# A wait on GpSimd for VectorE's attention shift, in a fused decoder layer on one core

## The reference

```python
# 1: linear attention, 32 heads of 8
qkv = relu(x @ W_qkv.T); q, k, v = split(qkv)
vk = [v | 1]^T k ;  z = vk q ;  y = (z[:8] / (z[8] + 1e-15)) @ W_p.T + b_p
x = layernorm(x + y)
# 2: cross attention to a context (16, 256, 256), 16 heads of 16, 2D rotary positions
q = rope(x @ Wq.T); k = rope(c @ Wk.T); v = c @ Wv.T
x = layernorm(x + softmax(q k^T / 4) v @ Wo.T + b_o)
# 3: low-rank feed-forward, 256 -> 64 -> 1024 -> 64 -> 256
x = layernorm(x + gelu(x @ U1 @ V1 + b1) @ U2 @ V2 + b2)
```

## Time and profile before

| | |
|---|---|
| median of three executions | 564.23 us |
| the profiled execution | 563.59 us |
| its span | 561.7 us |
| TensorE busy (matmuls) | 501.4 us, 89% of the span |
| VectorE busy | 427.0 us, 76% |
| GpSimd busy | 343.9 us, 61% |
| ScalarE busy | 312.5 us, 56% |
| mean granted TensorE clock | 0.967 of full speed (2.4 GHz) |

### The profile page before, as it was taken

How to read it: one execution, slowest core, us unless ns; L and a number is a source line. 1 busy time by engine, 2 the same in 40 slices (tenths; PEclk the granted TensorE clock), 3 DMA queues, 4 the chain that set the end, 5 groups by cost and what they waited for, 6 DMA issues and landing times.

```text
span 561.7 us, 11399 instructions
## 1 busy us (share of the span) xinstructions
PE 501.4 (89%) x4044; PEld 338.6 (60%) x4044; DVE 427.0 (76%) x878; ACT 312.5 (56%) x457; POOL 343.9 (61%) x391
## 2 busy tenths in 40 slices
PE   6997899998989898989898989898969678999992
PEld 3885666666676666666666767575746234545451
DVE  6567778888888888888888888888887767254554
ACT  3552366574647474747373747465646457656560
POOL 6558064858585867676767677676667334433435
PEclk9999799999999999999999999999999689999997
DMA  8553103011311132021203120302000001133332
GB/s 274 142 99 103 43 12 81 16 57 34 75 51 43 39 72 82 11 54 58 84 8 55 58 81 11 90 22 61 11 25 11 25 20 57 39 112 113 114 113 112
DMA packets 29131, 36.01 MB, mean 64 GB/s; under 512 B 5720, under 2 KB 15320, under 8 KB 29080
## 3 DMA queue, kind: packets, MB, share of 16 engines
q1 hardware_dynamic: 28216, 34.37, 21.6%
q10 hardware_dynamic: 864, 0.95, 0.6%
HBM read 23.51 MB, written 8.65 MB: 57 GB/s over the span
## 4 chain that ended last, share of the span: by engine, by line
PE 64%; DVE 17%; issue 9%; POOL 4%; ACT 4%; DMA 1%; POOLq 1%; SPq 0%; ACTq 0%
PE FR L1222 18%; PE BK L1222 12%; PE BK L1400 8%; PE SC L1381 5%; PE SC L1349 5%; DVE nmax L1037 5%; PE FR L1309 4%; PE FR L1301 3%; DVE shift L1047 3%; DVE nmax_c L1043 3%; PE FR L1286 3%; PE FR L1426 2%; POOL rs L647 2%; POOL c_fm L652 2%; DVE lin_fm_l L996 2%
## 5 line engine op out<-in xcount | busy, mean ns | idle before, releaser
L1037 DVE TENSOR_REDUCE nmax<-SC 128x4 f32<-128x1024 f32 x128 | 155.6, 1216 | 25.8 <-PE SC L1349 24.6
L755 ACT ACTIVATE probs<-SC 128x1024 f32<-128x1024 f32 x128 | 130.9, 1026 | 68.6 <-PE SC L1381 68.4
L1400 PE MATMUL BK<-probs,v_aug 128*32 128x256 f32 x1024 | 70.2, 393 | 0.3 <-DVE y L1087 0.3
L1349 PE MATMUL SC<-k_blk,q_grp 48*128 48x512 f16 x256 | 51.4, 398 | 7.9 <-DVE nmax L1037 7.0
L1381 PE MATMUL SC<-q_grp,k_blk 64*128 64x256 f16 x512 | 50.9, 279 | 5.2 <-ACT probs L755 2.5
L851 ACT ACTIVATE probs<-SC,b_ff 128x512 f32<-128x512 f32 x64 | 38.9, 688 | 25.9 <-PE SC L1591 25.9
L536 POOL TENSOR_TENSOR rs<-ve,minus_half 128x2 f32<-128x2 f32 x16 | 11.3, 706 | 52.5 <-DVE nm L1019 52.5
L1400 PEld LDWEIGHTS BK<-probs,v_aug 128*32 128x32 f32 x1024 | 27.0, 110 | 27.1 <-issue 12.3
L1381 PEld LDWEIGHTS SC<-q_grp,k_blk 64*128 64x128 f16 x512 | 20.0, 96 | 32.6 <-issue 15.4
L717 ACT ACTIVATE lin_fm_h<-FR 128x512 fp32r<-128x512 f32 x15 | 9.0, 597 | 46.0 <-PE FR L1309 46.0
L529 POOL TENSOR_TENSOR att_fm_l<-att_raw,att_fm_h 128x512 fp32r<-128x512 f32 x16 | 20.6, 1288 | 20.7 <-ACT att_fm_h L730 20.7
(11 more groups left out here) (239 smaller groups left out, 1588.4 us busy)
## 6 DMA issues: line engine op xcount, KB each, us to landing
x_fm<-in_x_fm SPq DMA_DIRECT2D x16, 256.0 KB, 5.9
x_tm<-in_x_tm SPq DMA_DIRECT2D x16, 256.0 KB, 5.4
x_kept<-x2b SPq DMA_DIRECT2D x16, 256.0 KB, 2.1
x_tm<-x_kept SPq DMA_DIRECT2D x16, 256.0 KB, 2.7
out<-c_fm SPq DMA_DIRECT2D x16, 256.0 KB, 2.0
c_fm<-in_c_fm SPq DMA_DIRECT2D x15, 256.0 KB, 5.3
tables<-rope_tables SPq DMA_DIRECT2D x16, 128.0 KB
k_blk<-k_rope SPq DMA_DIRECT2D x128, 16.0 KB, 1.8
```

Source lines behind the costliest of these rows:

```text
L755: act.activation(probs[:, j % 4], (SC[j % 2] if b == LAST else SB)[:], ACT.Exp, scale=SCALE).then_inc(s_exp, 1)
L1037: dve.tensor_reduce(nmax[:, t, :, 2 * q:2 * q + 2], src[:].rearrange("p (s f) t -> p s f t", s=2), AX.X, ALU.max, negate=True).then_inc(s_ ...
L1349: mm = pe.matmul(out[:, 2 * s:2 * s + 2].rearrange("p h t -> p (h t)"), q_grp[n % NB][rows, q, t * P:(t + 1) * P], k_blk[n % NB][rows, q]. ...
L1400: mm = pe.matmul(BK[q // 2][HP * k:HP * (k + 1), (q % 2) * T:(q % 2 + 1) * T], v_aug[b % NB][:, t, HC * q + k], probs[:, j % 4, k], start= ...
```

## The change

One line is added to GpSimd's step. After the last instruction of `rope_q(n)`, GpSimd waits until s_shift has reached b + 2, that is, until VectorE has finished shift(b+1) at the end of its own step b. Only then does it go on with `residual2(n)`, `keep_x2(q)` and `split_c(m)`. In steps without a block n (b = 14) there is no wait.

```diff
@@ -587,6 +587,7 @@
                     split_x(m + 1)
                 if on(n):
                     rope_q(n)
+                    pool.wait_ge(s_shift, b + 2)
                     residual2(n)
                 if on(q):
                     keep_x2(q)
```

## The result

| | before | changed |
|---|---|---|
| median of the first comparison | 563.96 us (4 runs) | 535.75 us (4 runs) |
| the changed kernel again, on another chip | 564.66 us (11 runs) | 537.50 us (6 runs) |
| the profiled execution | 563.59 us | 537.56 us |
| its span | 561.7 us | 535.8 us |
| ratio | | 0.9506, 95% interval 0.9481 to 0.9532; again: 0.9507, 0.9472 to 0.9542 |

The change makes the kernel 4.9% faster. The profiled execution lost 26.03 us; the medians lost 28.2 and 27.2. The prediction had 537.5 us, 26.1 less than the profiled execution before.

A forecast was written before the change was run, and what follows sets the result against it. The loop was bound by TensorE's queue plus one wait for VectorE's shift, held by GpSimd. Idle 24.5 plus overlap 2.1 less 0.5 for ve made 26.1 us, off the profiled 563.59: 537.5 us, range 533.5 to 545.

The forecast's parts named there:

- The rival that the shift is slow for a reason of its own: VectorE's shift: GpSimd contention is not the cause, so no change, 563.6 us; chance 0.02.
- The sum: Whole run: 24.5 us of TensorE idle plus 2.1 of overlap less 0.5 gives 26.1 us won.
- 0.15: TensorE, each of 14 changed steps: us won beyond the idle, because queued matmuls overlap; 2.1 us in all.
- ve's 0.5: VectorE's L1018 (128x2), held by GpSimd's cs_fm_l: 0.4 to 0.5 us late, counted in full once, behind b = 12.
- the spacing of the two score groups: TensorE: last scores start 0.23 us after block n1's first; the transposes should follow equally, so a step gains 2.07.
- The nearest row: VectorE's L1092 at 475.32, beside GpSimd's lin_tm: 0.34 instead of 0.17 us, so L1018 should also wait for GpSimd's end.
- The tail: GpSimd's held-back x1b, x2b, cs_fm_h and cs_fm_l: 4.46 us, running 273.80 to 278.26 behind the shift.
- The covers: Slack behind held work: costs 0; rs's 2.71 us just used up, VectorE's PSUM copy not held, ScalarE's copy 0.4 early.
- the rival of half a us a step: A hold reaches TensorE every step through L1018 or ScalarE's normalization: gain 20, time 543.5 us; chance 0.13.
- the one that all of VectorE's work is held: GpSimd's tail holds all VectorE work behind the shift: 0.4 us a step left, 558 us; chance 0.05.
- The slower rival: Shift, GpSimd's tail, rs, normalization, transposes become the loop once the tail takes 6.9 us; at 7.5, 572 us; chance 0.03.
- The clock: TensorE's clock falls near the end: if gone, 1 to 4 us more, outside the sum; 531 to 535, chance 0.09.

The follow-up runs named there:

- e2: Against the kernel before: the new wait one instruction later, behind x1b (residual2), leaving one GpSimd instruction beside the shift; 545.5 us, ratio 0.9694.
- e4: Against the kernel before, no wait: x1b and x2b each written by two 128x256 instructions instead of one 128x512; 549.96 us, ratio 0.9769.
- e1: Against the kernel before: the new wait behind split_c, so all four GpSimd instructions still run beside the shift; 564.23 us, ratio 1.0017.
- e3: Against the kernel before: the new wait behind keep_x2, leaving two GpSimd instructions (x1b, x2b) beside the shift; 558.7 us, ratio 0.9922.
- e6: Changed kernel with three extra unread 128x512 GpSimd additions behind x2b in steps b = 2 to 12; 564.26 us, ratio 1.0 to the kernel before.
- e7: Changed kernel with 30 extra unread matmuls in TensorE's waits of the last three steps, first run; 535.62 us, ratio 0.95 to the kernel before.
- e8: Apparently (by the order of the text) the changed kernel unaltered, run again on another chip; 537.50 us, ratio 0.9507 to the kernel before.

## Why the prediction was right

**The cause.** The shift's three operations each wait for the end of GpSimd's instruction in hand: shown by e2 to e4, with one, two, and half instructions beside them. The rival that the shift is slow for a reason of its own fell with them. That the wait itself does something is ruled out by e1, and by e3, where it held GpSimd and won no more than the one free operation. Which resource VectorE and GpSimd contend for no run here shows.

**The sum, part by part.** Every stretch between two transposes can be held against the one before. TensorE's transposes before that stand in no group above, then those after:

```profile
61.81 0.39 PE L1365 MATMUL FR<-ident,shift 128*128 128x128 f16 x2
...
111.84 0.29 PE L1365 MATMUL FR<-ident,shift 128*128 128x128 f16 x2 [0.91 <-DVE shift L1049]
...
385.78 0.28 PE L1365 MATMUL FR<-ident,shift 128*128 128x128 f16 x2 [1.92 <-DVE shift L1049]
412.74 0.28 PE L1365 MATMUL FR<-ident,shift 128*128 128x128 f16 x2 [1.47 <-DVE shift L1049]
```
```profile
61.65 0.28 PE L1366 MATMUL FR<-ident,shift 128*128 128x128 f16 x2
84.88 0.29 PE L1366 MATMUL FR<-ident,shift 128*128 128x128 f16 x2
109.32 0.28 PE L1366 MATMUL FR<-ident,shift 128*128 128x128 f16 x2
...
363.55 0.28 PE L1366 MATMUL FR<-ident,shift 128*128 128x128 f16 x2
389.00 0.28 PE L1366 MATMUL FR<-ident,shift 128*128 128x128 f16 x2
411.72 0.29 PE L1366 MATMUL FR<-ident,shift 128*128 128x128 f16 x2
431.69 0.28 PE L1366 MATMUL FR<-ident,shift 128*128 128x128 f16 x2 [0.30 <-DVE shift L1050]
```

| stretch, by the shift that ends it | won | expected |
|---|---|---|
| the second (to 86.44 before) | 1.40 | 1.34 |
| the third | 0.96 | 1.06 |
| the next ten, 27.4 each before | 19.71 | 20.6 |
| the one that shows 1.47 | 1.51 | 1.62 |
| the one that shows 1.84 (to 437.16) | 1.70 | 1.99, less ve's 0.5 |
| the last, and all behind it | 0.40 + 0.06 | 0 |
| ahead of the loop | 0.16 | 0 |

The column won adds to 25.9, the difference of the spans. The expected values are the idle of each place and 0.15. In ten steady steps 0.9 us is missing: there the prediction took 0.23 us from the start of the last scores to that of the transposes, the spacing of the two score groups. The trace after has 0.32 (261.54 to 261.86), so a step won 1.98, not 2.07. That is the one term that was mis-sized over the whole loop, by 4%. The trace before had it to be read: the second of two score groups is followed 0.31 later there.

```profile
279.11 0.38 PE L1349 MATMUL SC<-k_blk,q_grp 48*128 48x512 f16 x2
279.42 0.50 PE L1222 MATMUL FR<-w_kv_h,xs_fm_h 128*128 128x512 f32 x1
```

That the profiled execution lost 26.03 us where 26.1 was stated is in part luck: against the 0.9 too much stand 0.6 at the two ends, where 0 was put, and 0.2 in the stretch with ve. The medians, at 28.2 and 27.2, won one to two us more than the sum.

**ve.** The nearest row, 0.34 beside lin_tm, gave the right mechanism: 0.39 us now, ending 265.95 where cs_fm_l ends 265.93. It was put at 0.5 to 0.6, and 0.4 to 0.5 late; it is 0.2 late. The tail ends where it was put, 5.18 us behind the start of nmax_c (5.17 worked out). But ve starts 4.81 behind it and not 4.69: the prediction moved it by TensorE's 2.07, while by its own times for the copy VectorE's work ahead of ve moves by 1.99. In the steady step that costs nothing, as predicted. Where it was to count in full (417.82 in the earlier trace rows) TensorE now waits 2.48 instead of 2.63 us, and the stretch won 1.70. Without a hold of ve 1.99 was expected, so 0.29 is missing: the 0.09 above, and 0.19 by ve (0.36 us instead of 0.17), for which 0.5 was put.

**The covers.** L1055, the copy that reads PSUM, takes 0.68 us in the middle of x2b: no hold, as its 0.16 of overlap had suggested. The rs used its 2.71 up and has 0.17 left. ScalarE's copy ended half a us ahead of scores2(b, 0). With no wait of TensorE in a steady step, neither the rival of half a us a step nor the one that all of VectorE's work is held came true.

**The slower rival.** Its chain was right as far as GpSimd's tail, rs and ScalarE's normalization, and e6 made it the loop; but TensorE then waited for the exponential behind the normalization and for the split context, not for transposes. Its price was wrong: the prediction let a step turn slower at a tail of 6.9 us. With 8.46 us (246.08 to 254.54 in e6's trace) a step took 27.90 instead of 27.40, and the kernel, with the long tail in 11 of its 14 steps, was at 564.26, just level. One to one, that puts the turn at about 7.96 us, an estimate. What failed here is the cover, put at about 0.35 us. It is 1.54 us, and ScalarE's order behind mr ends it first.

**The clock.** The term left out of the sum, 1 to 4 us if the falls at the end disappear, did not come, since the falls did not go: they are still there in the profiled execution (0.83 from 410 to 430). Whether they are worth that much stays open; the one trace without them in the last steps, e7's, was 2.0 us shorter at the end, and the medians don't show it. Why the first four executions had a median 1.81 us under the profiled one, and the next six had not, stays open too. The ramp varies by as much: between the first two transposes lie 22.78 us in e8's trace and 24.78 in e7's.

## What to carry to other kernels

A tiny VectorE operation from SBUF to SBUF that takes a microsecond may not be slow but held by a GpSimd instruction: compare its end with the ends on GpSimd's timeline. If it sits on the path, hold back GpSimd work that has slack until it is done, or cut that work into shorter instructions; count the slack through every engine that waits for the held work in its own order, since the first cover to go may be two engines away. And the gain ends where the next queue is full: the shift came 2.42 us earlier, and TensorE, busy until then, could use 1.98 of it.

## What was not expected of the hardware

- VectorE gets its turn between two GpSimd instructions that run back to back, in every steady step, and its next operation then waits for the next one: 1.23, 1.19 and 0.56 us for operations of 0.18 or 0.19, about 0.65 each with half instructions. A chain of small dependent operations therefore paid once per operation.
- Of VectorE's work beside GpSimd's tail only ve was held (0.39 instead of 0.17). The copy out of PSUM (0.68), the addition with one operand in PSUM (0.69), the statistics (0.75 for two) and the row maxima (1.22) kept their times. Nor is every small operation from SBUF to SBUF held: the reciprocal of 128x32 took 0.34 us in the middle of a GpSimd instruction, as it took 0.35 at 474.00 in the trace before, with GpSimd idle. The held ones shown above are TENSOR_SCALAR and SCALAR_TENSOR_TENSOR.

```profile
271.84 0.34 DVE L1068 RECIPROCAL rden<-o_tok 128x32 f32<-128x32 f32 x1
```
```profile
271.11 1.16 POOL L490 TENSOR_TENSOR k_cos<-k,tables 128x512 f16<-128x512 f16 x1 [0.72 <-ACT k L704]
```
- A GpSimd instruction of 128x256 in such a pair took 0.71 us, over half of the 1.28 of 128x512: cutting one in two cost 0.14 us.
